# Output mixing of a tile in one turn, even experts left and odd experts right, and an output product over 128 rows

## The reference, cut to what matters

```
gate_o = jnp.einsum('btc,hec->bthe', x, Wd)
_, sel_o = jax.lax.top_k(gate_o, K)
mask_o = jax.nn.one_hot(sel_o, E, dtype=x.dtype).sum(axis=3)
res = jnp.einsum('bthe,bthd,efd->bthf', mask_o, attn, Wo)
return res.sum(axis=2)
```

## Time and profile before

| | |
|---|---|
| median of 3 runs | 3109.82 us (3106.86 to 3110.35) |
| the profiled execution | 3113.69 us, span 3111.7 us |
| TensorE matmul busy | 2559.5 us, 82% of the span, 14892 records |
| VectorE busy | 1570.6 us, 50% |
| ScalarE busy | 1367.7 us, 44% |
| GpSimd busy | 806.4 us, 26% |
| mean granted TensorE clock | 0.915 of full speed |

### The profile page before, as it was taken

How to read it: one execution, slowest core, us unless ns; L and a number is a source line. 1 busy time by engine, 2 the same in 40 slices (tenths; PEclk the granted TensorE clock), 3 DMA queues, 4 the chain that set the end, 5 groups by cost and what they waited for, 6 DMA issues and landing times. The chain is left out here.

```text
span 3111.7 us, 43916 instructions
## 1 busy us (share of the span) xinstructions
PE 2559.5 (82%) x14892; PEld 1579.8 (51%) x14892; DVE 1570.6 (50%) x2650; ACT 1367.7 (44%) x2945; POOL 806.4 (26%) x370
## 2 busy tenths in 40 slices
PE   4884699879897898879897898988988798986476
PEld 2353346554475445655365544754456544664254
DVE  4235753546635384454735465354834457336622
ACT  0232226553364525553364524555255533653254
POOL 1002620105501181013701064012800137004500
PEclk6896799989898998999999898989989899998699
DMA  2110010102001120012101020011200121001001
GB/s 73 41 48 8 10 51 1 55 15 72 16 15 41 41 59 2 15 55 55 33 7 49 14 76 12 15 41 41 59 2 15 55 55 32 15 14 39 1 28 31
DMA packets 210733, 101.59 MB, mean 33 GB/s; under 512 B 137367, under 2 KB 189620, under 8 KB 210492
## 3 DMA queue, kind: packets, MB, share of 16 engines
q1 hardware_dynamic: 205052, 95.74, 11.1%
q10 hardware_dynamic: 5440, 2.75, 0.3%
HBM read 77.48 MB, written 20.99 MB: 32 GB/s over the span
## 5 line engine op out<-in xcount | busy, mean ns | idle before, releaser
L690 POOL TENSOR_TENSOR prod<-pv,mixv 128x1024 f32<-128x1024 f32 x184 | 598.8, 3294 | 270.2 <-ACT pv L1133 163.2
L1510 DVE TENSOR_REDUCE nmax<-bank 128x1 f32<-128x512 f32 x512 | 341.3, 686 | 629.5 <-PE bank L972 628.1
L1169 ACT ACTIVATE prT<-bank 128x512 f32<-128x512 f32 x512 | 305.7, 597 | 615.6 <-PE bank L705 610.7
L972 PE MATMUL bank<-keys,qs 64*128 64x512 f32 x1024 | 324.5, 712 | 218.1 <-ACT pr L1182 99.0
L629 POOL TENSOR_TENSOR rstd<-vareps,minus_half 128x4 f32<-128x4 f32 x48 | 50.1, 1043 | 1511.6 <-DVE vareps L1279 1511.5
L1182 ACT ACTIVATE pr<-bank,nmax 128x512 f32<-128x512 f32 x512 | 349.7, 685 | 161.4 <-DVE nmax L1510 160.3
L705 PE MATMUL bank<-ident,pr 128*128 128x128 f32 x2048 | 362.9, 304 | 27.5 <-ACT prT L1169 27.5
L705 PEld LDWEIGHTS bank<-ident,pr 128*128 128x128 f32 x2048 | 246.6, 153 | 253.5 <-issue 201.9
L1075 ACT ACTIVATE arena<-bank 128x512 f32<-128x512 f32 x256 | 152.9, 597 | 461.9 <-PE bank L817 384.8
L1008 PE MATMUL bank<-prT,vals 128*64 128x128 f32 x4096 | 289.3, 285 | 40.1 <-ACT prT L1169 40.1
L1475 DVE TENSOR_REDUCE vals<-prod 128x128 f32<-128x1024 f32 x256 | 305.2, 1207 | 32.8 <-POOL prod L690 32.8
(11 more groups left out here) (220 smaller groups left out, 3188.2 us busy)
## 6 DMA issues: line engine op xcount, KB each, us to landing
Wg<-in_L_ffn_Wg SPq DMA_DIRECT2D x64, 256.0 KB, 2.7
Wu<-in_L_ffn_Wu SPq DMA_DIRECT2D x64, 256.0 KB, 3.1
Wd<-in_L_ffn_Wd SPq DMA_DIRECT2D x64, 256.0 KB, 3.8
out_rows<-on SPq DMA_DIRECT2D x32, 512.0 KB, 2.6
onR<-out_rows SPq DMA_DIRECT2D x32, 512.0 KB, 3.9
xin<-in_L_attn_x SPq DMA_DIRECT2D x8, 256.0 KB, 4.3
mask_rows<-masko SPq DMA_DIRECT2D x8, 256.0 KB, 4.3
maskR<-mask_rows SPq DMA_DIRECT2D x8, 256.0 KB, 6.9
```

The lines of the kernel that those rows point to most:

```text
L690: g.tensor_tensor(*value_piece(n), ALU.mult).then_inc(vprod_r[0], 1)
L972: pe.matmul((S0, S1)[(turn + odd) % 2][:, :], qs[half, j % 3, r, :], keys[half, p, :], start=True, stop=True).then_inc(s_ps[0], 1)
L1169: s.activation(prT[:, m % 3, :], TB[:, :], ACT.Copy).then_inc(pT_r[0], 1)
L1510: v.tensor_reduce(nmax[:, m % 2:m % 2 + 1], (S0, S1)[turn % 2][:, :], X_AXIS, ALU.max, negate=True).then_inc(nmax_r[0], 1)
```

## The change

A tile gets one mixed turn. Each group has two matmuls with the same weights `onR[:, g, :]`: one with the 32 columns of the even experts into partitions 0 to 63 of the bank, one with the 32 columns of the odd experts into partitions 64 to 127. The 16 groups fill the 512 columns of one bank. So `ymT`, `WoT` and `WoG` become 128 x 4 x 128 (even expert of a pair below, odd above), one ScalarE copy takes the whole bank, and the result step takes 4 matmuls over 128 rows. The mask sum on VectorE writes the experts in the order 0 2 4 6 1 3 5 7. In the setup the transposed weights are copied without splitting the halves. The list of steps has 4 mixed turns less a batch, so `heads` has 83 marks in place of 86 and `close` 4 in place of 5, and the interleaving with the other list shifts by as much.

```diff
-            steps += [("mixed", 2 * (i - 1)), ("mixed", 2 * i - 1)]
+            steps.append(("mixed", i - 1))
...
-    steps += [("mixed", 2 * (NT - 1)), ("mixed", 2 * NT - 1), ("rest", 0), ("result", NT - 1)]
+    steps += [("mixed", NT - 1), ("rest", 0), ("result", NT - 1)]
...
-        WoT = sb("WoT", [DS, NE, P])
-        WoG = sb("WoG", [DS, NE, P])
+        WoT = sb("WoT", [P, NE // 2, P])
+        WoG = sb("WoG", [P, NE // 2, P])
...
-        ymT = sb("ymT", [DS, NE, P])
+        ymT = sb("ymT", [P, NE // 2, P])
...
-                g.tensor_tensor(WoG[:, :, :], WoT[:, :, :], rows1b[0:DS, :].unsqueeze(1).to_broadcast([DS, NE, P]), ALU.mult).then_inc(WoG_r[0], 1)
+                g.tensor_tensor(WoG[:, :, :], WoT[:, :, :], rows1b[:, :].unsqueeze(1).to_broadcast([P, NE // 2, P]), ALU.mult).then_inc(WoG_r[0], 1)
...
-                        wait(pe, onR_in, b, 16 * (x // 2 + 1))
-                        wait(pe, spread_r, b, x // 2 + 1)
-                        for g in range(HALF):
-                            n = HALF * (x % 2) + g
-                            last = pe.matmul(bank_k[0:DS, g * NE * TG:(g + 1) * NE * TG], onR[:, n, :], spread[:, n, :], start=True, stop=True)
+                        wait(pe, onR_in, b, 16 * (x + 1))
+                        wait(pe, spread_r, b, x + 1)
+                        w = NE * TG // 2
+                        for g in range(OGN):
+                            for odd in range(2):
+                                last = pe.matmul(bank_k[DS * odd:DS * odd + DS, g * w:(g + 1) * w], onR[:, g, :], spread[:, g, w * odd:w * odd + w], start=True, stop=True, skip_group_check=True)
                         last.then_inc(s_ps[0], 1)
...
-                        for e in range(NE):
-                            last = pe.matmul(bank_k[:, 0:P], ymT[:, e, :], WoG[:, e, :], start=(e == 0), stop=(e == NE - 1))
+                        for e in range(NE // 2):
+                            last = pe.matmul(bank_k[:, 0:P], ymT[:, e, :], WoG[:, e, :], start=(e == 0), stop=(e == NE // 2 - 1))
...
-                        if x % 2 == 0 and x:
-                            wait(s, xout_r, b, x // 2)
-                        to = ymT[:, :, P // 2 * (x % 2):P // 2 * (x % 2 + 1)].rearrange("d e (g t) -> d g e t", t=TG)
-                        of = bank_k[0:DS, :].rearrange("d (g e t) -> d g e t", g=HALF, e=NE)
+                        if x:
+                            wait(s, xout_r, b, x)
+                        to = ymT[:, :, :].rearrange("d e (g t) -> d g e t", t=TG)
+                        of = bank_k[:, :].rearrange("d (g e t) -> d g e t", g=OGN, t=TG)
                         s.activation(to, of, ACT.Copy).then_inc(s_out[0], 1)
...
-                    elif 32 <= 4 * n + i < 36:
-                        for odd in range(2):
-                            last = v.tensor_copy(dst[:, odd, :], src[DS * odd:DS * odd + DS, :])
...
-                v.tensor_tensor(masko[:, :, :, :].rearrange("p i h e -> p (i h) e"), oh1[:, half:n, :], oh2[:, half:n, :], ALU.add).then_inc(masko_r[0], 1)
+                v.tensor_tensor(masko[:, :, :, :].rearrange("p i h (o a) -> p (i h) a o", o=2), oh1[:, half:n, :].rearrange("p n (a o) -> p n a o", o=2),
+                                oh2[:, half:n, :].rearrange("p n (a o) -> p n a o", o=2), ALU.add).then_inc(masko_r[0], 1)
```

More of the change, by code:

```diff
@@ L27 @@
 OGN = P // TG
-HALF = OGN // 2
 NBACK = HS // 2 // NJ
@@ L99 @@
 NCOPIED = COPIED[-1]
-BUILD_AT = {STEP_AT["mixed", 2 * i] - BUILD_BEFORE: i for i in range(NT)}
+BUILD_AT = {STEP_AT["mixed", i] - BUILD_BEFORE: i for i in range(NT)}
 MARKS["begin"] = BEGIN = 2
 MARKS["heads"] = FINISH_AT - BEGIN
-CLOSE_AT = STEP_AT["mixed", 2 * (NT - 1)]
+CLOSE_AT = STEP_AT["mixed", NT - 1]
 MARKS["finish"] = (CLOSE_AT - FINISH_AT + 1) // 2
@@ L432, in build @@
                  + [(raw_wv[:, i, :], WvT[:, i * P:(i + 1) * P]) for i in range(4)]
-                 + [(raw_wo[:, i, :], WoT[:, 2 * i:2 * i + 2, :]) for i in range(4)]
+                 + [(raw_wo[:, i, :], WoT[:, i, :]) for i in range(4)]
                  + [(raw_gates[:, i, :], gatesT[:, i * P:(i + 1) * P]) for i in range(2)]
@@ L978, in steps @@
                     if kind == "mixed":
-                        wait(pe, onR_in, b, 16 * (x // 2 + 1))
-                        wait(pe, spread_r, b, x // 2 + 1)
-                        for g in range(HALF):
-                            n = HALF * (x % 2) + g
-                            last = pe.matmul(bank_k[0:DS, g * NE * TG:(g + 1) * NE * TG], onR[:, n, :], spread[:, n, :], start=True, stop=True)
+                        wait(pe, onR_in, b, 16 * (x + 1))
[4 more added lines that the diff above has]
+                                last = pe.matmul(bank_k[DS * odd:DS * odd + DS, g * w:(g + 1) * w], onR[:, g, :], spread[:, g, w * odd:w * odd + w], start=True, stop=True, skip_group_check=True)
                         last.then_inc(s_ps[0], 1)
                     if kind == "result":
-                        wait(pe, s_out, b, COPIED[STEP_AT["mixed", 2 * x + 1]])
+                        wait(pe, s_out, b, COPIED[STEP_AT["mixed", x]])
                         wait(pe, WoG_r, b, 1)
-                        for e in range(NE):
-                            last = pe.matmul(bank_k[:, 0:P], ymT[:, e, :], WoG[:, e, :], start=(e == 0), stop=(e == NE - 1))
+                        for e in range(NE // 2):
+                            last = pe.matmul(bank_k[:, 0:P], ymT[:, e, :], WoG[:, e, :], start=(e == 0), stop=(e == NE // 2 - 1))
                         last.then_inc(s_ps[0], 1)
@@ L1514, in steps @@
                         if i:
-                            wait(v, s_ps, b, TURN[STEP_AT["mixed", 2 * i - 1]])
+                            wait(v, s_ps, b, TURN[STEP_AT["mixed", i - 1]])
                         v.tensor_tensor(spread[:, :, :].rearrange("p g (e t) -> p (g e) t", t=TG),
```

## The result

The changed kernel takes 3076.04 us (median of 7 runs, 3067.76 to 3091.9), the kernel before, run beside it, 3106.86 us. The ratio is 0.9912 with a 95% interval of 0.9887 to 0.9937: some 27 us less (30.8 between the two medians), where the prediction had 50. The time is inside the wide range of 3040 to 3108 us and just outside the forecast's own, 3042 to 3075. The profiled execution took 3074.05 us.

A forecast was written before the change was run, and what follows sets the result against it. TensorE's queue, or a TensorE-ScalarE-TensorE loop through the score banks, mostly sets the pace. Six full batches 36 us, batch 6: 6.4, batch 7: 6.3, setup 1.2, together 50: 3110 to 3060; own range 3042 to 3075, wide range 3040 to 3108.

The forecast's parts named there:

- Loads into two halves side by side: Mixing: loads into left and right column halves run in parallel, so 64 loads take 1.9 us, the same as before.
- Halves in turn: Rival, mixing: load side is shared, 64 loads take 3.7 us, total 3112, no change; 3100 to 3125, chance 0.17.
- issue binds: Rival, mixing: sequencer can't issue a load and matmul every 0.029 us; 3.7 us more at 26 places, 3156; chance 0.11.
- Output product 0.9 a tile: Output product: half the loads, 1.78 us to 0.89, saving 0.9 at full clock and 1.8 at half clock.
- Step taken out, 0.9 at tiles 0 and 2, nothing at tile 1: Head loop: one step fewer between mixing and next scores, counted 0.9 us at tiles 0 and 2, 0 at tile 1.
- Tile 3 in the expert stage, 1.5: Closing part: smaller product and a mark fewer start value pieces earlier; 1.0 to 3.5 us possible, 1.5 taken.
- Batch 7, 6.3: Last batch, heads alone: three tiles at 1.8 us and 0.9 for the last product, 6.3 saved.
- Small edits: Setup: four WoT copies in place of eight save 1.2 us; WoG and the mask sum's strided store counted 0.
- No wait is added: Whole program: no wait is added, and the number of exponent and Gelu swaps stays the same; no time counted.
- Absorbed: Rival: halves parallel, but front work, gates' chain and value pieces take up TensorE's savings; 3088, 3076 to 3100, chance 0.17.

The follow-up runs named there:

- two-turn kernel: Changed kernel's new layout, but again two mixed turns a tile, 8 groups each, two copies, marks as before the change: 3069.06 us, ratio 0.9861.
- e6_rest_close_only: Changed kernel with an empty step where the second mixed turn was, in `close` alone: 3095.58 us, ratio 0.9954.
- e5_rest_heads_only: Changed kernel with an empty step where the second mixed turn was, in `heads` alone: 3041.16 us, ratio 0.9777.
- e8_empty_mark_before_scores: Changed kernel with no empty step, but an unused mark between each mixing in `heads` and the scores behind it: 3041.18 us, ratio 0.9782.
- e9_top_later: Changed kernel with VectorE's first maximum over the gates one mark later: 3058.75 us, ratio 0.9853.
- e10_rest_and_top_later: Changed kernel with the empty step in `heads` and VectorE's first gate maximum one mark later: 3009.51 us, ratio 0.9675.

## Why the prediction came out as it did

- **Loads into two halves side by side**: right. 1.95 us for 64 loads, 2.06 with the matmuls, as forecast (1.9), 3.7 when they aren't alternated. *Halves in turn* and *issue binds* fall: a matmul record every 0.032 us is sustained. The Trainium skill (page TensorE: Matmul & The Clock Gate, section "Wait — 56ns, not 53.3ns?") gives some 62 ns for each matmul when the sequencer's own code decodes it. That would have made 4.0 us; this trace doesn't agree, so that case isn't this one, and the 0.058 us of the kernel before lay under 62 ns already.
- **Output product 0.9 a tile**: right in sum (0.9 and, cold, 1.8 a tile counted, at least 28 us over 32 tiles; 31.7 measured), not in every place. Doubling it costs some 0.9 at tiles 1, 2 and 3 of a full batch and nothing at tile 0, where the change gave 0.14. Not all of the 31.7 is placed.
- **Step taken out, 0.9 at tiles 0 and 2, nothing at tile 1**: the places were wrong, the size in one. From the first mixing to the next scores at tile 0 it is now 3.82 us (predicted 3.7 to 4.5). Tile 0 gave 1.65, tile 2 lost 0.88, tile 1 gave 2.1, most of it also with two turns, so that there it is not the step. Against the two-turn kernel one turn with an empty step is worth 1.2 at tile 0 and nothing at the two others.
- **Tile 3 in the expert stage, 1.5**: the mechanism was right (the product, 1.3 by the 104.5 us of `e6_rest_close_only`, and a mark fewer for the rest), the size too small: 2.7 to 3.8 in each of six batches, near the upper bound of 3.5 that was worked out for VectorE and GpSimd as the bound, 7 to 14 us more than counted.
- **Batch 7, 6.3**: 0.2 less in this profile (164.1 to 163.9, with two short stretches at the 1.2 GHz level, at 2969 and 3013 us, that before has not) and 3.6 less in the second one (160.5, with one such stretch); the second one also begins the batch with some 5 us at that level, the other two with 10 to 11. Either way 6.3 was too much. In heads 26 to 28, with the product of tile 0, the gap is 0.49 shorter after the change and 0.93 with the empty step. The empty step takes no turn, so the banks alternate the same in both: the missing 0.44 comes from the step that is no longer there and not from the banks, and the 0.9 counted for it at each tile of this batch did not come.
- **Small edits**: the first expert stage, behind the setup, ends at 178.6 and 180.6 us in the two profiles, 183.4 before: 3 to 5 us and not 1.2. The four copies of WoT take 0.87 us, 1.5 less than the eight; the mean granted clock up to there is 0.84 and 0.82, 0.81 before, so part of the rest may be the clock. The mask sum, taken at no change, costs 0.27 us more each time.
- **"No wait is added"**: this is the step that failed. No semaphore is added, but the prediction looked at what the missing marks do in `close` alone; in `heads` it called 83 in place of 86 a matter of their number. They put VectorE's gate reductions ahead of the emptying of a score bank at two places of each full batch. That costs 37 us (`e5_rest_heads_only`, `e8_empty_mark_before_scores`), some 28 of them, by the estimate above, as the wait itself and the rest with a lower clock in that stretch. Without it the change would have given 67 to 69, above the 50 counted. So two errors of opposite sign, some 18 us too small and 37 not seen, leave the forecast about 20 off. That the measured time still lies in the wide range is owed to this and to the rivals that the range took in; as an account of the mechanism it is luck.
- **Absorbed (3076 to 3100)** has the measured time at its edge, but not the reason: the gain was not lost at the places where it arose, save tile 0's product; it was there and was paid out at two others.

What stays open: the gate maximum doesn't explain all of the 37 us. With it moved in both orders (`e9_top_later`, `e10_rest_and_top_later`) the orders differ by 49. The profile places part of the rest at L1433, 2.9 us a batch where the clock stays full and 4.3 where it falls, but no kernel moved L1433 alone, and none held the clock fixed. Nor is it shown why the setup gained more than its copies.

## What to carry to other kernels

When an edit takes a step out of a list by which several engines' programs are interleaved, write down both orders and look at every place where an instruction that waits for another engine moves in front of one that empties a shared buffer: that cost here 37 us, more than the whole edit brought. An empty step or an unused mark that restores the old order separates the worth of the work removed from that of the order, in one run; its place matters as much as its presence. Before a cost is put down to a wait, the granted clock of the same stretch is to be read in several batches. And narrow matmuls that fill both column halves did best with their weights sent to the halves in alternation: 2.06 us for the block, 3.71 with one half after the other.

## What was not expected of the hardware

Alternating halves sustain a 64-column load and a 32-column fp32 matmul record every 0.032 us, against 0.058 for the blocks in one half. The same program had TensorE at the 1.2 GHz level for 501.5 us in one execution and 549.0 in the next; its seven first runs go from 3067.76 us at a mean granted clock of 0.922 to 3091.9 at 0.910, the longer the lower. In one execution, the same stretch of a batch took 39.6 us with 3.4 us at that level and 45.7 with 23.9. A VectorE addition of 512 fp32 elements on each partition whose store has a stride took 1041 ns in place of 775.
